# Halved norm matmuls, small-tile masks and new engine orders in a fused diffusion-block kernel

## The reference, cut to what matters

```python
qkv = shift(x) @ Wqkv                      # 16 heads of 64
q = rotary(l2norm(q) * qs) * scale
k = rotary(l2norm(k) * ks) / scale
# windows of 32 queries, each with its own and the previous window's keys (64)
sim = where(mask, -max, q @ k.T * 8)
x = softmax(sim) @ v @ Wo + x
x = (a * gelu(gate)) @ W2 + b2 + x         # a, gate = layernorm(shift(x)) @ W1 + b1
```

## Time and profile before

| | before |
|---|---|
| median of 3 runs | 3449.61 us (3441.67 to 3456.11) |
| profiled execution, its own time | 3448.65 us |
| profiled execution, span | 3446.9 us |
| busy PE, PEld | 3333.7 us (97%), 2469.4 us (72%) |
| busy ACT, DVE, POOL | 2701.8 us (78%), 2439.3 us (71%), 1445.0 us (42%) |
| mean granted TensorE clock | 0.991 |
| DMA, mean over the span | 122 GB/s |

### The profile page before, as it was taken

One profiled execution on the slowest core, in us unless ns is written; L12 is line 12 of the kernel. 1 busy time (PEld: TensorE's weight loads), 2 busy tenths in 40 slices (PEclk: granted clock), 3 DMA queues, 4 the chain that ended last, 5 costly groups with the idle time before them and its releaser, 6 DMA issues.

```text
span 3446.9 us, 152524 instructions
## 1 busy us (share of the span) xinstructions
PE 3333.7 (97%) x63228; PEld 2469.4 (72%) x63228; DVE 2439.3 (71%) x5141; ACT 2701.8 (78%) x9033; POOL 1445.0 (42%) x1276
## 2 busy tenths in 40 slices
PE   7789999999999999999999999999999999999997
PEld 4457777777777777777777777777777777777775
DVE  5667777777777777777777777777777767777773
ACT  5667887878787787878788787877878787887875
POOL 2244443444444354444444443453434444443441
PEclk9999999999999999999999999999999999999998
DMA  2056655665655666565565655565565656556563
GB/s 73 1 109 132 131 123 126 134 136 115 147 118 125 129 137 132 128 131 123 120 148 117 139 128 128 122 138 127 121 141 120 132 127 133 122 121 136 114 135 75
DMA packets 361274, 421.43 MB, mean 122 GB/s; under 512 B 52291, under 2 KB 265814, under 8 KB 359814
## 3 DMA queue, kind: packets, MB, share of 16 engines
q1 hardware_dynamic: 360582, 411.67, 55.2%
HBM read 19.30 MB, written 2.10 MB: 6 GB/s over the span
## 4 chain that ended last, share of the span: by engine, by line
PE 70%; POOL 18%; issue 4%; DVE 2%; ACT 1%; DMA 0%; SPq 0%; POOLq 0%; DVEq 0%
PE ring_ps L1234 16%; POOL qs L617 13%; PE out_ps L1326 12%; PE out_ps L1336 10%; PE ring_ps L1279 8%; PE small_ps L1245 6%; PE score_ps L1297 4%; PE ring_ps L1308 4%; PE ring_ps L1372 4%; POOL probs L601 3%; DVE prod L993 2%; PE ring_ps L1269 2%; PE out_ps L1350 2%; PE score_ps L1289 1%; PE small_ps L1253 1%
## 5 line engine op out<-in xcount | busy, mean ns | idle before, releaser
L774 ACT ACTIVATE probs<-score_ps,neg_max,rq 128x64 f32<-128x64 f32 x3072 | 1194.7, 420 | 95.7 <-DVE neg_max L1031 94.5
L993 DVE TENSOR_TENSOR prod<-ring_ps,tables 128x512 f32<-128x512 f32 x1536 | 956.9, 680 | 285.6 <-PE ring_ps L1234 257.8
L617 POOL TENSOR_TENSOR ks<-prod 128x1024 f32<-128x1024 f32 x192 | 452.7, 2358 | 852.5 <-DVE prod L993 852.4
L1234 PE MATMUL ring_ps<-xs,wqk 128*128 128x256 f32 x3072 | 768.9, 388 | 15.5 <-issue 10.6
L774 ACT ACTIVATION_READ_ACCUMULATOR probs<-score_ps,neg_max,rq 128x1 f32 x3072 | 677.1, 220 | 0.0
L730 ACT ACTIVATE square<-ring_ps,biases 128x512 f32<-128x512 f32 x768 | 516.9, 687 | 197.2 <-DVE prod L993 196.0
L1234 PEld LDWEIGHTS ring_ps<-xs,wqk 128*128 128x128 f32 x3072 | 571.1, 191 | 104.3 <-issue 17.6
L601 POOL TENSOR_TENSOR probs<-probs,inv_sums 128x512 f32<-128x512 f32 x384 | 401.1, 1045 | 576.0 <-DVE inv_sums L1045 576.0
L617 POOL TENSOR_TENSOR qs<-prod 128x1024 f32<-128x1024 f32 x192 | 453.4, 2361 | 395.4 <-DVE prod L993 395.4
L1326 PEld LDWEIGHTS out_ps<-pt,v 64*64 64x64 f32 x24576 | 397.0, 135 | 113.5 <-issue 111.6
L763 ACT ACTIVATE att_t<-out_ps 128x512 f32<-128x512 f32 x384 | 217.0, 591 | 297.3 <-PE out_ps L1326 297.2
(11 more groups left out here) (182 smaller groups left out, 3835.6 us busy)
## 6 DMA issues: line engine op xcount, KB each, us to landing
v<-vs SPq DMA_DIRECT2D x1344, 128.0 KB
qt<-qs SPq DMA_DIRECT2D x768, 128.0 KB
kt<-ks SPq DMA_DIRECT2D x768, 128.0 KB
v<-vs SPq DMA_DIRECT2D x192, 64.0 KB
wqk<-in_L_ffn_Wqkv SPq DMA_DIRECT2D x6, 1024.0 KB, 5.1
wv<-in_L_ffn_Wqkv SPq DMA_DIRECT2D x6, 512.0 KB, 5.8
wo<-in_L_ffn_Wo SPq DMA_DIRECT2D x6, 512.0 KB
out_dram<-ks SPq DMA_DIRECT2D x16, 128.0 KB, 1.9
```

The lines of the kernel that those rows point to most:

```text
L617: pool.tensor_tensor(dst, prod_a[p % 2], prod_b[p % 2], ALU.add).then_inc(rot_ready, 1)
L774: last = nc.scalar.activation(probs[i][:, j, e, :], score_ps[e][:, KEYS * j:KEYS * (j + 1)], ACT.Exp, bias=neg_max[:, h:h + 1], scale=rq[p ...
L993: last = V.tensor_tensor((prod_b if a else prod_a)[p % 2][:, f, :] .rearrange("p (u c) -> p u c", u=2), bank[:, :].rearrange("p (u c) -> p ...
L1234: last = mm(bank_of(s)[:, TOKENS * f:TOKENS * (f + 1)], wqk[:, n, 2 * c + f, a, :], xs[:, WINDOW:PADDED], start=True, stop=True)
```

## The change

Six edits, all in the main loop. The squares of both halves are added on POOL (new steps AS0 to AS3, 128x512 each), and NK and NQ run one matmul for each quad instead of two. The mask becomes 32 queries by 64 keys with a selector, and is put in by eight matmuls of 64 rows by 32 columns instead of two of the whole array. The split norms are padded with zeros from 48 to 128 columns, so TU and KN use the whole array. `pt` gets a second buffer. All orders are written anew, which also changes who shares a bank. One small constant more is loaded at the start.

```diff
 PE_ORDER = """
-PA0 PB0 PA1 S00 S01 PB1 BI WO PA2 NK CEN PB2 VAR PA3 PB3 TK UP0 UP1 S10 S11 V0 UP2 T00 TU NQ KN0 PAD V1 PV00 KN1
-TQ T01 V2 DN T10 PV01 V3 T11 PV10 PV11
+PA0 BI S00 S01 PB0 PA1 PB1 WO PA2 CEN PB2 PB3 VAR NK S10 S11 TK PA3 UP0 UP1 T00 UP2 TU V1 V3 KN0 KN1 PV00 T01 DN
+PAD NQ PV01 V0 T10 V2 TQ T11 PV10 PV11
 """
 DVE_ORDER = """
-XS RA0 RB0 RA1 M0 RB1 BI XA XB AR00 RA2 RB2 CK XG RB3 RA3 H0 M1 AR01 H1 TC00 UC H2 KM0 CQ VC1 KM1 AR10 TC01 X
-AR11 TC10 VC3 TC11
+XS RA0 M0 BI RB0 RA1 RB1 XA AR00 RA2 XB RB2 RB3 CK XG AR01 M1 RA3 H0 TC00 H1 UC H2 VC1 VC3 KM0 KM1 TC01 X AR10
+AR11 CQ TC10 TC11
 """
 ACT_ORDER = """
-QA0 QB0 QA1 E00 QB1 E01 E02 SQ QA2 LN E03 QB2 RTK LG G0 QB3 QA3 G1 VC0 G2 LE E10 E11 E12 E13 VC2 OC00 OC01 OC10
-RTQ OC11
+QA0 E00 E01 QB0 QA1 E02 QB1 SQ E03 LN QA2 QB2 RTK LG G0 QB3 QA3 G1 G2 LE E10 E11 E12 E13 OC00 VC0 OC01 RTQ VC2
+OC10 OC11
 """
 POOL_ORDER = """
-AD0 AD1 AD2 AN00 AD3 RK TB0 AN01 TB1 AN10 TB2 AN11 TB3
+AD0 AD1 AS0 AS1 AD2 AN00 RK AD3 TB0 AN01 TB1 TB2 AS2 AS3 AN10 TB3 AN11
 """
 SP_ORDER = """
-LS LK MQ MK LV LL MV
+LS LK MQ MK LV MV LL
...
+                if kind == "AS":
+                    p = s[1]
+                    last_square = max(rank(ACT_ORDER, (x, p), "QA", "QB") for x in ("QA", "QB"))
+                    pool.wait_ge(sq_ready, at(g, QK_BANKS, last_square + 1))
+                    one, other = square[p % COUPLES]
+                    pool.tensor_tensor(one[:, :], one[:, :], other[:, :], ALU.add).then_inc(sq_summed, 1)
...
-                    turn = bank_of(("TU",))[0:3 * HEADS, 0:TOKENS // 2].bitcast(BF16)
+                    turn = bank_of(("TU",))[:, 0:TOKENS // 2].bitcast(BF16)
...
-                    dve.wait_ge(pv_ready, at(g, TILES, i))
-                    V.tensor_copy(pt[:, 4 * c:4 * c + 4, :], bank_of(("T", i, c))[:, :].rearrange("p (j c) -> p j c", c=P)
+                    if g > 0:
+                        dve.wait_ge(pv_ready, at(g - 1, TILES, i + 1))
+                    V.tensor_copy(pt[i][:, 4 * c:4 * c + 4, :], bank_of(("T", i, c))[:, :].rearrange("p (j c) -> p j c", c=P)
...
-                    pe.wait_ge(sq_ready, at(g, QK_BANKS, last_square + 1))
+                    pe.wait_ge(sq_summed, at(g, 2 * COUPLES, COUPLES * (n + 1)))
                     pe.wait_ge(norms_ready, at(g, 2, n))
-                    for a in range(2):
-                        for u in range(QUADS):
-                            last = mm(norm2_ps[WINDOW * u:WINDOW * (u + 1), :], head_ones[:, :],
-                                      square[u // 2][a][:, TOKENS * (u % 2):TOKENS * (u % 2 + 1)],
-                                      start=(a == 0), stop=(a == 1), skip_group_check=True)
+                    for u in range(QUADS):
+                        last = mm(norm2_ps[WINDOW * u:WINDOW * (u + 1), :], head_ones[:, :],
+                                  square[u // 2][0][:, TOKENS * (u % 2):TOKENS * (u % 2 + 1)],
+                                  start=True, stop=True, skip_group_check=True)
...
-                        for e in range(2):
-                            if e == 1 and i == 0:
-                                pe.wait_ge(q_moved, moved(g, 1))
-                            mm(score_ps[e][:, :], ident_bf[:, :], mask_bf[:, i, :, :].rearrange("p j c -> p (j c)"),
-                               start=True, stop=False, skip_group_check=True)
+                        for w in range(WPT):
+                            for e in range(2):
+                                if (w, e) == (WPT - 1, 1) and i == 0:
+                                    pe.wait_ge(q_moved, moved(g, 1))
+                                mm(score_ps[e][WINDOW * w:WINDOW * (w + 1), :],
+                                   mask_sel_bf[64 * e:64 * e + 64, int((i, w) == (0, 0)), :],
+                                   mask_bf[64 * e:64 * e + 64, :, :].rearrange("p j c -> p (j c)"),
+                                   start=True, stop=False, skip_group_check=True)
```

More of the change, by code:

```diff
@@ L32 @@
 MOVES = 8
+RK_PARTS = P // HEADS
 V_MOVES = 16
@@ L138, in build @@
         ident_bf = sb("ident_bf", [P, P], BF16)
[L139 removed]
+        mask_bf = sb("mask_bf", [P, PAIRS, KEYS], BF16)
+        mask_sel_bf = sb("mask_sel_bf", [P, 2, WINDOW], BF16)
         head_ones = sb("head_ones", [P, WINDOW])
[L141 removed]
+        head_sel_bf = sb("head_sel_bf", [P, QUADS, P], BF16)
         rotary = sb("rotary", [P, 2, 2, TOKENS])
@@ L187, in build @@
         inv_sums = [sb(f"inv_sums{i}", [P, PAIRS, 2]) for i in range(TILES)]
-        pt = sb("pt", [P, PAIRS, P])
+        pt = [sb(f"pt{i}", [P, PAIRS, P]) for i in range(TILES)]
         att_t = sb("att_t", [P, PAIRS, TOKENS])
@@ L280, in build @@
         mod_a = carve(P, BATCH, 6)
-        mask = carve(P, TILES, KEYS)
-        head_sel = carve(3 * HEADS, QUADS, P)
+        mask = carve(P, KEYS)
+        mask_sel = carve(P, 2, WINDOW)
+        head_sel = carve(P, QUADS, P)
         wmod = carve(P, 6 * DIM)
@@ L310, in build @@
             sem("f_" + n) for n in ("qkv sq eps inv q2 k2 v kcol max kmax log r qfin kv kvt qt qtc kw kg y gw xb x1").split())
-        xs_ready, proj_ready, prod_ready, sq_ready, rot_ready, v_made, v_even_ready, v_odd_ready = (
-            sem(n) for n in ("xs_ready", "proj_ready", "prod_ready", "sq_ready", "rot_ready", "v_made",
+        xs_ready, proj_ready, prod_ready, sq_ready, sq_summed, rot_ready, v_made, v_even_ready, v_odd_ready = (
+            sem(n) for n in ("xs_ready", "proj_ready", "prod_ready", "sq_ready", "sq_summed", "rot_ready", "v_made",
                              "v_even_ready", "v_odd_ready"))
@@ L439, in _ @@
             load_x(2)
-            for dst, src in ((mask[:, :, :], t["mask"]), (head_ones[:, :], t["head_ones"]),
+            for dst, src in ((mask[:, :], t["mask"]), (mask_sel[:, :, :], t["mask_sel"]), (head_ones[:, :], t["head_ones"]),
                              (head_sel[:, :, :], t["head_sel"]), (rotary[:, :, :], t["rotary"])):
@@ L552, in _ @@
             pool.tensor_copy(head_sel_bf[:, :, :], head_sel[:, :, :])
-            for i in range(TILES):
-                for j in range(PAIRS):
-                    last = pool.tensor_copy(mask_bf[:, i, j, :], mask[:, i, :])
+            pool.tensor_copy(mask_sel_bf[:, :, :], mask_sel[:, :, :])
+            for j in range(PAIRS):
+                last = pool.tensor_copy(mask_bf[:, j, :], mask[:, :])
             last.then_inc(consts_ready, 1)
@@ L1257, in step @@
                     bank_free(g, s)
-                    turn = bank_of(s)[0:3 * HEADS, 0:TOKENS // 2].bitcast(BF16)
+                    turn = bank_of(s)[:, 0:TOKENS // 2].bitcast(BF16)
                     for i in range(TILES):
@@ L1401, in shape_constants @@
     rotary = np.stack([f.T for f in four], 1).astype(np.float32).reshape(P, 2, 2, TOKENS)
-    query = np.arange(P)[:, None] % WINDOW
+    query = np.arange(WINDOW)[:, None]
     key = np.arange(KEYS)[None, :]
-    hidden = (key > query + WINDOW) | (query > key)
-    mask = np.zeros((P, TILES, KEYS), np.float32)
-    for i in range(TILES):
-        no_window = (i == 0) & (np.arange(P)[:, None] < WINDOW) & (key < WINDOW)
-        mask[:, i] = np.where(hidden | no_window, MASKED, 0.0)
+    mask = np.zeros((2, 64, KEYS), np.float32)
+    mask[:, 0:WINDOW] = np.where((key > query + WINDOW) | (query > key), MASKED, 0.0)
+    mask[:, WINDOW] = np.where(key < WINDOW, MASKED, 0.0)
+    mask_sel = np.zeros((2, 64, 2, WINDOW), np.float32)
+    mask_sel[:, 0:WINDOW] = np.eye(WINDOW, dtype=np.float32)[:, None, :]
+    mask_sel[:, WINDOW, 1] = 1.0
     head_ones = np.zeros((P, WINDOW), np.float32)
-    head_sel = np.zeros((HEADS, QUADS, P), np.float32)
+    head_sel = np.zeros((RK_PARTS, HEADS, QUADS, P), np.float32)
     for r in range(4):
@@ L1413, in shape_constants @@
         for u in range(QUADS):
-            head_sel[4 * u + r, u, HALF * r:HALF * (r + 1)] = 1.0
-    return {"ident": np.eye(P, dtype=np.float32), "mask": mask, "head_ones": head_ones,
-            "head_sel": np.concatenate([head_sel] * 3), "rotary": rotary,
+            head_sel[0:3, 4 * u + r, u, HALF * r:HALF * (r + 1)] = 1.0
+    return {"ident": np.eye(P, dtype=np.float32), "mask": mask.reshape(P, KEYS), "mask_sel": mask_sel.reshape(P, 2, WINDOW), "head_ones": head_ones,
+            "head_sel": head_sel.reshape(P, QUADS, P), "rotary": rotary,
             "biases": np.tile(np.array([LN_EPS, 0.0], np.float32), (P, 1)),
```

15 lines of the change are left out of this document (7 added, 8 removed).

## The result

The changed kernel takes 3599.4 us (median of 4 runs, 3587.17 to 3607.5) against 3451.07 us for the kernel before on the same chip (4 runs). The ratio is 1.043, with a 95% interval of 1.0392 to 1.0468. The forecast was 3358 us in a range of 3290 to 3400, so sign and size are both wrong.

The account below looks back on a forecast made before the run. PE was taken as the bound: its work falls 1.65 to 31.45 us, 31.9 with waits, tied with the DMA loop at 32.0. Mean period 32.44 against 33.49; 96 x -1.05 + 10 = -91 gives 3358 us, range 3290 to 3400.

Parts of the forecast that it names:

- the DMA chain: Loop from scores through M1, RA3, AD3, MQ and MK to the next scores: 32.0 us, a tie with PE.
- S00 to MQ: Part of the DMA loop from the start of the scores to MQ's first issue: 19.1 us.
- The prediction's own sign of being wrong: PE waiting more than 1 us a period for any one releaser, or the mask line taking over 0.5.
- the 13.9: PE's steps from the start of scores S00 to the end of scores S11, added up: 13.9 us.
- the DMA chain is longer: Rival: MQ and MK back to back land later; 1 us more a period leaves no gain; 3385 to 3460, chance 0.18.
- Norms: NK and NQ on PE: half of the matmul rounds go, 0.43 us each, -0.86 a period.
- KN and TU: Norm turns on PE: whole-array steps following others pay no switch, -0.3 us a period.
- the switch: PE going between small tiles of different shapes, NK into S10 and NQ into PV01: 0.1 us each, +0.2.
- PE's own odd stalls stay: Disturbed periods: PE's stalls unchanged, so 0.39 us kept, with 0.05 added for DMA stalls.
- PE is the bound: there is next to no idle time to win: Main loop: PE busy 33.05 of 33.10 us in an undisturbed period, so only less PE work shortens it.
- POOL holds DVE: Rival: M1's neg_max is held by AN00 on POOL; 0.3 us for a partial catch, up to 1.0; chance 0.06.
- The mask tiles run one after another: Rival: the eight mask matmuls run in turn, 1.7 us instead of 0.43, some 3610 us; chance 0.03.

Follow-up runs that it names:

- e1: The changed kernel with only one of the eight DMAs of each of MQ and MK, so most of their data is not moved: 3436.69 us.
- e6: The changed kernel with scores S00 and S01 two steps later in PE's order, M0 and ACT's squares moved to match: 3433.67 us.
- e9: The changed kernel with scores S00 and S01 one step later in PE's order, behind PB0 only, M0 and two ACT steps moved to match: 3498.5 us.
- e3: The changed kernel with its new orders but without the adds on POOL; NK and NQ keep both matmuls per quad: 3608.93 us.
- e4: The changed kernel with the old orders and no adds, keeping small-tile masks, whole-array norm turns and the second pt: 3424.69 us.
- e15: e10 with the whole-array masks of the kernel before: 3425.11 us.
- e12: The kernel before with the small-tile masks alone: 3457.19 us, ratio 1.0023.
- e14: e4 with RK ahead of AD3 in POOL's order: 3442.97 us.
- e7: The changed kernel with only one of MQ's eight DMAs, so most of qt is not moved, and MK whole: 3488.06 us.
- e10: e6 with the next layer's tables behind the adds of q on POOL instead of before them: 3424.35 us.
- e13: e14 with the adds for q alone; NQ goes behind KN1, TQ ahead of T11, CQ behind KM1: 3467.1 us.

## Why the prediction was wrong

**The step that failed** is the DMA chain: "this loop and PE are a tie at 31.9 to 32.0". It was the right loop, and it was sized 3.2 us short (2.8 against the forecast mean period of 32.44). The measured terms: S00 to MQ 20.33 for 19.1 (+1.2), MQ's issues 5.95 for 5.33 (+0.6), MK's 6.12 for 5.50 (+0.6), landing and start 2.68 for 1.9 (+0.8). The prediction's own sign of being wrong came true: PE waits 1.4 us a period for one releaser, `kt`. e1, e6 and e9 show that the loop sets the period, e3 that the adds are not its cause.

The +1.2 lies in PE's work from S00 to the end of S11, which took a mean of 15.0 for the 13.9 that were counted; M1, RA3 and AD3 behind it took what they were given. The 13.9 are the steps of a quiet period put in a row. Over all periods this stretch holds 0.46 of "issue" idle and 1.5 us at the lower clock in the kernel after. A wait for `kt` lowers the clock of the work behind it, which is in the same loop. But e1, which has no such wait and 0.3 at the lower clock, has 0.69 of "issue" idle and takes 15.0 as well; its 23 periods with neither take 14.2. So the stretch doesn't shorten when the wait goes, and what the low clock alone adds stays open. Of the adds about 0.2 is in the term: in e3 NK has 0.43 more to do and waits for no add, and the term is 20.53. They take 1.27 each for the estimated 1.05; the 128x512 row that this was read from is AN, a multiply with a broadcast operand, and no add.

The three DMA terms were read in one quiet period too. Where the trace of before gave another figure (issues in 6.09, landing 10.1 after the first), the prediction made it a rival, with 18% and a price of at most 1 us. The means of before (5.56 and 5.61) were there to be worked out and would have added 0.3. The rise from these to 5.95 and 6.12 can be read from single issues. Most take 0.60, in every run. Those over 0.8 are 198 of 1536 in the kernel after and 102 before, and what they take beyond 0.60 is 0.81 and 0.95 a period for MQ and MK, against 0.42 and 0.45: the whole rise. Of the 198, 195 end 0.2 to 0.5 us after a block of instructions has landed on the queue q8, which is explained below; of the 1338 shorter ones 6 do. The timing says that an issue is held up while such a block comes, and more of MQ's and MK's issues now meet one (201 end so, 134 before). That MQ and MK follow one another doesn't explain it: MQ, which comes first, rose as well.

**Rival "the DMA chain is longer"**: this mechanism, beyond its priced size. Its own condition, "from 1.0 us on this rival decides for no gain", points the right way; at 3.2 us it decides for a loss. Its chance of a loss was 0.03.

**PE's work, term by term.** Norms: -0.86 forecast, 83.3/96 = -0.87 measured. KN and TU: -0.3 forecast, (17.4 + 1.8)/96 = -0.2 measured by busy time. But KN's 17 are not the padding: with it and the old orders (e4) KN stays at 75.7, and with the new orders and no adds (e3) it is 58.1. V's 26 in addition were not forecast: 12 come in e4, the rest with the new orders. Masks and small tiles show in PE's timeline of the kernel after:

```profile
1724.53 0.59 PE L1365 MATMUL out_ps<-xc_sq,mean_ones 128*128 128x256 f32 x2
1725.31 0.64 PE L1253 MATMUL small_ps<-square,head_ones 128*32 128x256 f32 x8 [0.19 <-POOL square L618]
1725.88 0.41 PE L1298 MATMUL score_ps<-mask_bf,mask_sel_bf 64*32 64x512 bf16 x8
1726.10 1.36 PE L1308 MATMUL score_ps<-kt,qt 64*32 64x64 f32 x116
1727.97 0.33 PE L1308 MATMUL score_ps<-kt,qt 64*32 64x64 f32 x12 [0.51 <-issue]
```

The mask takes 0.22 from its start to the scores (0.29 forecast), so its saving was 0.07 larger than forecast. The Trainium skill ("TensorE: Matmul & The Clock Gate", Part 3) gives 4 ns for each further tile, by which it would be 0.24: nearer than my 12 ns. NK takes 0.57, two rounds of 0.217 and 0.14 of overhead, as forecast, and neither it nor the mask behind it holds the further 0.1 that had been taken for the switch. The Trainium skill ("TensorEngine Tiling (Array Packing)", Key Properties) has a drain at every change of mode; between these two small shapes the trace shows no time for one, unless it is in the 0.14. The sum held for a quiet period: 31.9 forecast, 32.1 in e1. That is in part luck, since KN, V and the masks came out otherwise than counted.

**What the sum of PE did not hold** is "issue" idle. It rose from 21 to 71 (86 in e1), 0.5 to 0.7 a period, where "PE's own odd stalls stay" had been assumed. The last row above shows it: the scores stop for 0.51 with nothing to wait for. The trace tells what was missing. The page of the kernel after has a queue for instructions (packets, MB, share of 16 engines):

```profile
q8 instruction: 496, 8.13, 1.0%
```

These are blocks of 16 KB. In every run there is one for about 256 matmuls and weight loads, so they are mostly PE's own instructions. In the kernel after PE has 65 stops of this kind, 71.4 us in all, and every one ends 1.1 to 1.6 us after a block has landed; moved by a random time, 9% would. In e1 all of 96 do, and in the kernel before all of 29 (the latest at 1.62). In the rows above the block landed at 1726.57, and the scores went on at 1727.97. So PE stood because its next instructions had come late. The idle time falls with whole-array masks (65 to about 32 in e15) and rises with small ones (21 to 41 in e12), but the new orders raise it too: e4, with small masks and the old orders, has 33. Why the blocks come late in one order and not in another was not tested.

**"PE is the bound: there is next to no idle time to win"** was also half true. PE at 100% of a quiet period says that no other loop is longer, not that none is as long. The chain of before had 18% POOL in it. e4 and e12 (TU for RK, 0.3 a period), e14 (KN for UC, 0.4) and e7 (MK for KM1) show loops that stand close behind PE. This is why even e4, with PE 59 us less busy (3274.6), won 25.

**The small steps.** CEN waits 0.25 for XA (0.3 forecast). NQ waits at the change of layer, up to 3.03 us at once (3.1 forecast); e10, which removes most of it, wins 9 (10 forecast). "POOL holds DVE" did not come here: none of 192 `neg_max` is over 0.177 us in the kernel after. In e14 and e13 it did, in nearly every period.

```profile
L1041 DVE SCALAR_TENSOR_TENSOR neg_max<-row_max,rq x192: 174/176/177, 201.3 to 3556.5; 128x16 f32<-128x16 f32 x192
```

"The mask tiles run one after another" did not come either.

**Open.** Why the blocks of instructions meet more of MQ and MK in the new orders, and come late to PE more often. How much the low clock costs: a mean of 0.967 between levels of 1 and 0.5 is 238 us at the low one, against 62 before, and half of the extra 176 (88) is an upper bound; e1 with 103 of such time shows that most of it goes when the wait goes. How the some 30 us of e4 against e12 divide between the turns and the second `pt` is open; the prediction had 0 for the second.

## What to carry to other kernels

Where an order is written anew, count each loop that closes over a DMA queue from its means over all periods, issue and landing alike, and take a tie between two loops for a loss: a stretch counted from the steps of a quiet period left out 1.1 us of a mean period here. Before work saved on a busy engine is credited, read the chain of waits for a second engine with a share in it; it takes over as soon as the first is faster. When such a loop has become too long, the cheapest repair is to let it enter the order later: two steps were worth 166 us here, with no instruction changed.
